# Perceiver block on one core: key weights and chunk 1 moved forward at the start, one accumulator loaded earlier at the end

## The chip, the core and the metric

The kernel runs on 1 core of a Trainium2 chip. The core has TensorE (PE), VectorE (DVE), ScalarE (ACT), GpSimd (POOL) and a sequencer that issues DMAs (SP). They run their own instruction streams and meet through semaphores. Time is device microseconds (us); the kernel before takes 1537.28 us (median of 3 runs, 1536.81 to 1538.84).

## The reference, cut to what matters

Inputs are `x` (8 x 64 tokens of 512) and a context `ctx` (8 x 1601 x 512), all fp32. Three blocks follow each other, each with a residual:

```python
x = x + xattn(layernorm(x), ctx, ctx)   # 16 heads of 32: softmax(Q K^T / sqrt(32)) V, then W_O
x = x + attn(layernorm(x))              # x + differential attention over the heads of a token,
                                        # then layernorm and a 512-2048-512 feed forward with ReLU
x = x + ffn(layernorm(x))               # 32 experts, 6 per token (4 of 8 groups), SwiGLU of 256,
                                        # plus a shared expert of 512
# in xattn:  Q = x_q @ W_Q + b_Q;  K = ctx @ W_K + b_K;  V = ctx @ W_V + b_V
# in ffn:    out = sum over the 6 chosen experts of weight * down(silu(gate(x)) * up(x)) + shared(x)
```

The change lies in the preparation of Q and of the first keys, and in the last sum of `ffn`.

## The kernel before, in words

Matmuls of the cross attention are fp32 products made of three passes: each operand is split into a high part (`*_hi`, rounded to fp32r) and a low part (`*_lo`, the rest), and `mm3` (L65 to L67) adds hi*hi, hi*lo and lo*hi. So every loaded operand needs two instructions before PE can use it: a copy into the high part and a subtraction for the low part.

The context of one batch row is loaded transposed in 4 chunks of 402 columns (`c_raw`, 804 KB each; chunks are numbered 0 to 3). At the start ACT and DVE split chunk 0, and POOL splits chunks 1 to 3 by `split(b, c)` (L294 high, L297 low); POOL waits for `split_done` of chunk 0 first. Key step n (0 to 7) of a half of the heads multiplies chunk n // 2 by 128 columns of W_K: 12 matmuls of 402 columns into PSUM bank n % 3. ACT then adds the bias and rounds (`kT_hi`, L592), DVE makes the low part (`kT_lo`, L733), and that frees the bank: step n waits for the low part of step n - 3.

The queries of all tokens are prepared once. DVE normalises `xn` (statistics L977 to L984, a square root on ACT at L707, L986 to L989), PE transposes it in 16 pieces (L569), ACT and DVE split the transposed `xnT` (L713, L995) and the weights `wq` (L709, L997), and after key step 3 PE makes the projection in 48 matmuls. ACT and DVE split the result (`q_hi` L719, `q_lo` L1012), SP stores it and reads it back in the layout `qbd` (L263, L196). Before `q_hi` the scaled bias `bqs` must be there (L1008), and DVE makes two small selection matrices `sel` (L1000, L1001). The order on each engine is simply the order in which the code is written; nothing is scheduled by a planner. The same holds for the queue of SP, in which the loads are issued one after the other.

Then a loop over 8 batch rows and two halves of the heads does values, scores, softmax and the weighted sum, and in the gaps the key steps of the next half. Two further stages follow: the rest of the second block, and the routing with the experts. In the expert stage PE, DVE, ACT, SP and POOL run a loop of 6 expert blocks of 128 tokens per turn. POOL's scatter (L1691) adds the 128 result rows of a block to one of two accumulators in HBM, `acc0` for even and `acc1` for odd blocks. At the end SP waits for both accumulators (L1665 to L1667), loads four 128-row tiles of each (L1670, 256 KB each), DVE adds the pairs (L1870) and SP stores them (L1673). The tile `part` that receives the loads lies over the expert stage's working tile `e_mix`: `part[:, 0]` over the results `y` of blocks 0 to 3, `part[:, 1]` over the results of blocks 4 and 5 and what follows them.

Of the kernel before, what the change touches and what calls it, by code (L numbers as in the profile page):

```python
# [69 lines left out]
def queries_and_cross_attention(nc, a, keep):  # L70
# [6 lines left out]
    with ExitStack() as ctx:  # L77
# [304 lines left out]
        def _(pe):  # L382
# [181 lines left out]
            pe.wait_ge(ident_loaded, 16)  # L564
            for k in range(KD):
                for t in range(TT):
                    if k == 0:
                        pe.wait_ge(xn_done, t + 1)
                    ins = nc.tensor.transpose(ps[:, 4 + k, P * t:P * t + P], xn[:, t, P * k:P * k + P], ident[:])  # L569
                ins.then_inc(tr_full, 1)  # L570
# [17 lines left out]
        def _(act):  # L588
# [140 lines left out]
        def _(dve):  # L729
# [1418 lines left out]
```

## Time and profile before

| what | value |
|---|---|
| runs of the kernel before | 1537.28 us (1536.81 to 1538.84) |
| profiled execution, its own time | 1538.13 us |
| its span, mean granted clock of PE | 1536.2 us, 0.979 |
| busy: PE, PE weight loads, DVE, ACT, POOL | 95%, 78%, 55%, 36%, 37% |
| c_hi on POOL (L294), 31 of them, mean | 2905 ns |
| kT_lo on DVE (L733), 128 of them, mean | 635 ns |
| kT_hi (L592), q_hi (L719), square root (L707) on ACT at the start | 598, 690, 201 ns |
| bytes: a chunk; x, half of wkv, wq; an accumulator tile | 804 KB; 1024 KB each; 256 KB |
| expert weights w_gu, issue to landing, median of 49; the last | 7.9 us; 7.5 us |
| reload of the queries, 8 DMAs, issue to landing | 2.0, 2.2, 2.4 us (least, median, most) |
| DMA engines busy at 1520-1522, 1522-1524, 1524-1526, 1526-1528 us | 0.97, 0.61, 0.06, 0.96 |

Busy time is the time in which an engine executes. PE's busy time includes pipelined matmuls, whose ends are modelled, so rows of PE are read by their starts. In a timeline, brackets give the idle time before an instruction and what ended it. The mean busy share hides that the two ends of the program look different from the middle.

### The profile page before, as it was taken

How to read it: one execution, taken by the hardware profiler on the slowest of the kernel's cores; microseconds unless marked ns; L12 is line 12 of the kernel's file. 1: busy time of each engine (PE TensorE's matmuls, PEld its weight loads, DVE VectorE, ACT ScalarE, POOL GpSimd, SP SyncE). 2: the span in 40 equal slices, each digit the busy share in tenths (PEclk: the TensorE clock that was granted, in tenths of full speed). 3: DMA queues.
4: the chain of work that ended last, by engine and by line, in shares of the span. 5: the costliest groups of instructions: out<-in, count | busy, mean ns of one | idle time of the engine just before them, and what ended most of it. 6: DMA issues, size and time to landing. Idle time of an engine off the chain costs nothing. (4 is left out here: it accounts for less than half of the span.)

```text
span 1536.2 us, 23747 instructions
## 1 busy us (share of the span) xinstructions
PE 1464.4 (95%) x8826; PEld 1191.7 (78%) x8826; DVE 844.1 (55%) x2161; ACT 549.2 (36%) x1022; POOL 565.4 (37%) x276
## 2 busy tenths in 40 slices
PE   5999999999999999999999999788998989999994
PEld 4999999989999999899989999636665445555552
DVE  6455555544586755488655578739402634444442
ACT  3344345344354354443444533522211012222331
POOL 5006006006366604374811554526400124444442
PEclk9999999999999999999999999989997999999997
DMA  5102003013003013002112200350004659999999
GB/s 197 63 4 90 5 4 121 4 62 94 26 5 97 3 71 118 28 4 65 33 48 92 78 1 1 148 249 1 1 0 158 229 179 333 350 331 341 332 338 301
DMA packets 63976, 176.97 MB, mean 115 GB/s; under 512 B 15110, under 2 KB 32006, under 8 KB 54028
## 3 DMA queue, kind: packets, MB, share of 16 engines
q1 hardware_dynamic: 53708, 151.57, 27.7%
q0 software_dynamic: 10176, 24.12, 6.4%
q8 instruction: 64, 1.05, 0.3%
q14 instruction: 28, 0.23, 0.0%
HBM read 156.00 MB, written 19.66 MB: 114 GB/s over the span
## 5 line engine op out<-in xcount | busy, mean ns | idle before, releaser
L65 PE MATMUL ps_x<-wkv_hi,c_hi 128*128 128x256 f32 (+1 forms) x832 | 241.2, 290 | 0.0
L67 PE MATMUL ps_x<-wkv_hi,c_lo 128*128 128x256 f32 (+1 forms) x832 | 234.2, 282 | 0.0
L66 PE MATMUL ps_x<-wkv_lo,c_hi 128*128 128x256 f32 (+1 forms) x832 | 234.2, 281 | 0.0
L294 POOL TENSOR_TENSOR c_hi<-c_raw,ones 128x1608 fp32r<-128x1608 f32 x31 | 90.1, 2905 | 344.8 <-DMA c_raw<-ctxT 344.8
L769 DVE TENSOR_TENSOR pT<-ps_x,pT 128x512 fp32r<-128x512 f32 (+1 forms) x224 | 145.1, 648 | 123.3 <-ACT pT L617 120.6
L65 PE MATMUL ps_x<-c_hi,wkv_hi 128*128 128x402 f32 x512 | 195.7, 382 | 2.9 <-POOL c_lo L297 2.3
L617 ACT CAST pT<-ps_x 128x512 fp32r<-128x512 f32 (+1 forms) x224 | 124.5, 556 | 167.4 <-PE ps_x L472 164.4
L67 PE MATMUL ps_x<-c_hi,wkv_lo 128*128 128x402 f32 x512 | 177.9, 347 | 0.0
L66 PE MATMUL ps_x<-c_lo,wkv_hi 128*128 128x402 f32 x512 | 177.8, 347 | 0.0
L65 PEld LDWEIGHTS ps_x<-wkv_hi,c_hi 128*128 128x128 f32 (+1 forms) x832 | 153.5, 184 | 17.0 <-issue 17.0
L598 ACT CAST vv<-ps_x 128x512 fp32r<-128x512 f32 (+1 forms) x112 | 62.1, 555 | 278.5 <-PE ps_x L67 278.5
L1937 PE MATMUL ps_e<-e_w_gu,e_xT 128*128 128x512 f32 x344 | 157.1, 600 | 0.0
L67 PEld LDWEIGHTS ps_x<-wkv_hi,c_lo 128*128 128x128 f32 (+1 forms) x832 | 153.6, 185 | 0.0
L66 PEld LDWEIGHTS ps_x<-wkv_lo,c_hi 128*128 128x128 f32 (+1 forms) x832 | 153.2, 184 | 0.0
L313 POOL TENSOR_TENSOR x_tok<-t_q,t_k 128x1024 f32<-128x1024 f32 x48 | 114.2, 2397 | 101.0 <-PE ps_x L524 58.2
L739 DVE TENSOR_TENSOR vv<-ps_x,vv 128x512 fp32r<-128x512 f32 (+1 forms) x112 | 72.9, 651 | 138.9 <-ACT vv L598 138.9
L487 PE MATMUL ps_x<-pT,vv 128*128 128x256 f32 (+1 forms) x832 | 138.0, 287 | 4.8 <-DVE pT L769 4.4
L487 PEld LDWEIGHTS ps_x<-pT,vv 128*128 128x128 f32 (+1 forms) x832 | 125.8, 189 | 10.6 <-DVE pT L769 7.6
L733 DVE SCALAR_TENSOR_TENSOR kT_lo<-ps_x,bk,kT_hi 128x402 fp32r<-128x402 f32 x128 | 81.1, 635 | 95.9 <-ACT kT_hi L592 95.4
L752 DVE TENSOR_SCALAR_CACHE_REDUCE prob<-ps_x 128x402 f32<-128x402 f32 (+1 forms) x256 | 131.2, 569 | 0.0
L472 PE MATMUL ps_x<-ident,prob 128*128 128x128 f32 (+1 forms) x832 | 127.9, 273 | 0.0
L1691 POOL DMA_INDIRECT acc<-e_mix,e_row_out x42 | 66.3, 1579 | 144.7 <-DVE e_row_in L1747 120.7
(314 smaller groups left out, 2685.6 us busy)
## 6 DMA issues: line engine op xcount, KB each, us to landing
e_w_gu<-w_gu SPq DMA_DIRECT2D x49, 1024.0 KB, 7.9
c_raw<-ctxT SPq DMA_DIRECT2D x32, 804.0 KB, 5.0
e_w_dn<-w_dn SPq DMA_DIRECT2D x48, 512.0 KB, 5.6
x_tok<-slabs SPq DMA_DIRECT2D x13, 1024.0 KB, 4.8
spare<-slabs SPq DMA_DIRECT2D x8, 1024.0 KB, 11.1
h_late<-slabs SPq DMA_DIRECT2D x4, 1024.0 KB, 16.6
e_mix<-shared SPq DMA_DIRECT2D x2, 1536.0 KB, 8.5
wkv_raw<-w_qkv SPq DMA_DIRECT2D x2, 1024.0 KB, 12.3
```

Of the source, the lines that this page charges most:

```text
L65: nc.tensor.matmul(out, a_hi, b_hi, start=start, stop=False)
L66: nc.tensor.matmul(out, a_hi, b_lo, start=False, stop=False)
L67: return nc.tensor.matmul(out, a_lo, b_hi, start=False, stop=stop)
L294: nc.gpsimd.tensor_tensor(c_hi[:, :, chunk(c)], c_raw[:, :, chunk(c)], ones[:, 0:1].unsqueeze(2).to_broadcast([P, KD, CW]), ALU.mult).then ...
L313: nc.gpsimd.tensor_tensor(slab[:, 2 * D * (i % 2):2 * D * (i % 2) + 2 * D].rearrange("p (a b d) -> p a b d", a=2, b=2 * H2), q[:, 2 * i:2 ...
L472: ins = nc.tensor.transpose(ps[0:r, 6 + n % 2, c:c + P], prob[:, 2 * g + j, P * st:P * st + r], ident[:])
L487: ins = nc.tensor.matmul(ps[:, 4 + g, 256 * j:256 * j + 256], vv[0:r, st, 2 * g + j].rearrange("p l c -> p (l c)"), pT[0:r, n % 2, st % 2, ...
L617: nc.scalar.copy(pT[0:r, n % 2, 0:w, :, 0].rearrange("p a j c -> p (a j) c"), ps[0:r, 6 + n % 2, 0:256 * w].rearrange("p (a c) -> p a c", ...
L733: nc.vector.scalar_tensor_tensor(kT_lo[:, m, chunk(c)], ps[:, n % KEY_BANKS, 0:CW], bk[:, 2 * h + m:2 * h + m + 1], f32(kT_hi[:, m, chunk( ...
L752: ins = nc.vector.tensor_scalar(prob[:, p, CW * n:CW * n + w], ps[:, 2 * (i % 2) + j, 0:w], 0.0, None, ALU.add, ALU.max, accum_out=pmax[:, ...
L769: nc.vector.tensor_tensor(pT[0:r, n % 2, 0:w, :, 1].rearrange("p a j c -> p (a j) c"), ps[0:r, 6 + n % 2, 0:256 * w].rearrange("p (a c) -> ...
L1937: ins = nc.tensor.matmul(ps[:, GU], xT[:, b, P * g:P * g + P], w_gu[:, b, g], start=(g == 0), stop=(g == KD - 1))
```

## The change: what it does

- SP loads the key half of `wkv_raw` first, then chunk 0 and x; chunk 3 is issued before the value half of `wkv_raw`.
- ACT makes `wkv_hi` first, then the high part of chunk 0, `wq_hi`, the square root and the high part of chunk 1 (which POOL did; POOL leaves it out at (0, 1)). It takes the keys of steps 0 and 1 before `xnT_hi`.
- DVE makes `wkv_lo` first; it takes the keys of steps 0 and 1 right behind the normalised x, then `wq_lo` (which stood behind `xnT_lo`), `xnT_lo`, the keys of steps 2 and 3, and only then `sel`.
- PE does key steps 0 and 1, then the 16 transposes, then key steps 2 and 3.
- At the end SP issues the four loads of `acc0` when `acc0` is complete and `acc1` lacks only its last scatter. The loads of `acc1` follow when the last scatter has landed, each behind the landing of its `acc0` partner.

```diff
@@ sync
+            sp.dma_start(wkv_raw[:, :, 0:D], a["w_qkv"][1]).then_inc(wkv_loaded[0], 16)
             load_chunk(0, 0)
             sp.dma_start(xn[:], a["x"].rearrange("(t p) d -> p t d", p=P)).then_inc(qx_loaded, 16)
-            sp.dma_start(wkv_raw[:, :, 0:D], a["w_qkv"][1]).then_inc(wkv_loaded[0], 16)
...
             load_chunk(0, 2)
+            load_chunk(0, 3)
             sp.dma_start(wkv_raw[:, :, D:], a["w_qkv"][2]).then_inc(wkv_loaded[1], 16)
-            load_chunk(0, 3)
@@ gpsimd, split(b, c)
-                nc.gpsimd.tensor_tensor(c_hi[:, :, chunk(c)], c_raw[:, :, chunk(c)],
-                                        ones[:, 0:1].unsqueeze(2).to_broadcast([P, KD, CW]), ALU.mult).then_inc(split_hi, 1)
+                if (b, c) != (0, 1):
+                    nc.gpsimd.tensor_tensor(c_hi[:, :, chunk(c)], c_raw[:, :, chunk(c)],
+                                            ones[:, 0:1].unsqueeze(2).to_broadcast([P, KD, CW]), ALU.mult).then_inc(split_hi, 1)
@@ tensor (the 16 transposes went behind key step 1)
             for n in range(8):
                 for half in range(2):
                     keys(0, 0, n, half)
+                if n == 1:
+                    pe.wait_ge(ident_loaded, 16)
+                    for k in range(KD):
+                        for t in range(TT):
+                            if k == 0:
+                                pe.wait_ge(xn_done, t + 1)
+                            ins = nc.tensor.transpose(ps[:, 4 + k, P * t:P * t + P], xn[:, t, P * k:P * k + P], ident[:])
+                        ins.then_inc(tr_full, 1)
@@ scalar
+            act.wait_ge(wkv_loaded[0], 16)
+            nc.scalar.copy(wkv_hi[:, :, 0:D], wkv_raw[:, :, 0:D]).then_inc(wkv_hi_done, 1)
             act.wait_ge(c_loaded[0], 16)
             nc.scalar.copy(c_hi[:, :, chunk(0)], c_raw[:, :, chunk(0)]).then_inc(split_hi, 1)
...
+            act.wait_ge(c_loaded[1], 16)
+            nc.scalar.copy(c_hi[:, :, chunk(1)], c_raw[:, :, chunk(1)]).then_inc(split_hi, 1)
             act.wait_ge(bk_loaded, 16)
+            for n in range(2):
+                keys(0, 0, n)
             for m in range(KD):
                 act.wait_ge(tr_full, m + 1)
                 nc.scalar.copy(xnT_hi[:, m], ps[:, 4 + m]).then_inc(xT_hi_done, 1)
-            for n in range(4):
+            for n in range(2, 4):
                 keys(0, 0, n)
@@ sync, the end
-            for i in range(2):
-                wait_turn(sp, added[i], n * (16 * U // 2) + 16)
+            wait_turn(sp, added[0], n * (16 * U // 2) + 16)
+            wait_turn(sp, added[1], n * (16 * U // 2))
+            for t in range(TT):
+                sp.dma_start(part[:, 0, t], a["acc0"][P * t:P * t + P]).then_inc(part_loaded[t], 16)
+            wait_turn(sp, added[1], n * (16 * U // 2) + 16)
             wait_turn(sp, hid_done, n * U + 1)
             for t in range(TT):
-                for i in range(2):
-                    sp.dma_start(part[:, i, t], a[f"acc{i}"][P * t:P * t + P]).then_inc(part_loaded[t], 16)
+                sp.wait_ge(part_loaded[t], 16)
+                sp.dma_start(part[:, 1, t], a["acc1"][P * t:P * t + P]).then_inc(part_loaded[t], 16)
```

ACT at the start of the program, before. `q_std` is the square root, `q_wq_hi` the high part of the query weights, `q_xnT_hi` that of the transposed x.

```order
L703 CAST c_hi<-c_raw 128x4x402 [waits x_c_loaded0]
L705 CAST wkv_hi<-wkv_raw 128x4x512 [waits q_wkv_loaded0]
L707 ACTIVATE q_std<-q_veps 128x4 [waits q_step]
L709 ACTIVATE q_wq_hi<-q_wq_raw 128x2048 [waits q_w_loaded]
L713 CAST q_xnT_hi<-ps_x 128x512 [waits q_tr_full,q_bk_loaded]
L713 CAST q_xnT_hi<-ps_x 128x512 [waits q_tr_full] x3
L592 ACTIVATE kT_hi<-ps_x,bk 128x402 [waits x_k_full] x4
```

The same stretch of ACT, now.

```order
L705 CAST wkv_hi<-wkv_raw 128x4x512 [waits q_wkv_loaded0]
L707 CAST c_hi<-c_raw 128x4x402 [waits x_c_loaded0]
L709 ACTIVATE q_wq_hi<-q_wq_raw 128x2048 [waits q_w_loaded]
L711 ACTIVATE q_std<-q_veps 128x4 [waits q_step]
L713 CAST c_hi<-c_raw 128x4x402 [waits x_c_loaded1]
L594 ACTIVATE kT_hi<-ps_x,bk 128x402 [waits x_k_full,q_bk_loaded]
L594 ACTIVATE kT_hi<-ps_x,bk 128x402 [waits x_k_full]
L719 CAST q_xnT_hi<-ps_x 128x512 [waits q_tr_full] x4
L594 ACTIVATE kT_hi<-ps_x,bk 128x402 [waits x_k_full] x2
```

The weights went ahead of chunk 0, the square root went behind `q_wq_hi`, the copy of chunk 1 came in, and two of the four keys went ahead of `q_xnT_hi`.

DVE behind the statistics of x, before. `q_xn` is the normalised x, `sel` the selection matrices, `bqs` the scaled query bias.

```order
L989 TENSOR_SCALAR q_xn<-q_xn,q_mv,q_rstd 128x512 x3
L992 TENSOR_TENSOR wkv_lo<-wkv_raw,wkv_hi 128x4x512 [waits q_wkv_hi_done]
L995 TENSOR_TENSOR q_xnT_lo<-ps_x,q_xnT_hi 128x512 [waits q_xT_hi_done] x4
L997 SCALAR_TENSOR_TENSOR q_wq_lo<-q_wq_raw,q_wq_hi 128x2048 [waits q_wq_hi_done]
L1000 MEMSET sel 128x64 [waits q_ident_loaded]
L1001 TENSOR_TENSOR sel<-ident 128x64
L1000 MEMSET sel 128x64
L1001 TENSOR_TENSOR sel<-ident 128x64
L733 SCALAR_TENSOR_TENSOR kT_lo<-ps_x,bk,kT_hi 128x402 [waits x_k_hi_done,q_bk_loaded]
L733 SCALAR_TENSOR_TENSOR kT_lo<-ps_x,bk,kT_hi 128x402 [waits x_k_hi_done] x3
L1008 TENSOR_SCALAR bqs<-bq 128x4 [waits q_bq_loaded]
```

The same stretch of DVE, now.

```order
L997 TENSOR_SCALAR q_xn<-q_xn,q_mv,q_rstd 128x512 x3
L739 SCALAR_TENSOR_TENSOR kT_lo<-ps_x,bk,kT_hi 128x402 [waits x_k_hi_done,q_bk_loaded]
L739 SCALAR_TENSOR_TENSOR kT_lo<-ps_x,bk,kT_hi 128x402 [waits x_k_hi_done]
L1005 SCALAR_TENSOR_TENSOR q_wq_lo<-q_wq_raw,q_wq_hi 128x2048 [waits q_wq_hi_done]
L1008 TENSOR_TENSOR q_xnT_lo<-ps_x,q_xnT_hi 128x512 [waits q_xT_hi_done] x4
L739 SCALAR_TENSOR_TENSOR kT_lo<-ps_x,bk,kT_hi 128x402 [waits x_k_hi_done] x2
L1013 MEMSET sel 128x64 [waits q_ident_loaded]
L1014 TENSOR_TENSOR sel<-ident 128x64
L1013 MEMSET sel 128x64
L1014 TENSOR_TENSOR sel<-ident 128x64
L1016 TENSOR_SCALAR bqs<-bq 128x4 [waits q_bq_loaded]
```

`wkv_lo` left this stretch (it stands ahead of the low part of chunk 0 now), the keys went ahead of `sel`, and `q_wq_lo` went ahead of `q_xnT_lo`.

## Rows read from the trace of the kernel before

**Rows 1.** Windows: stretch, its us, busy us of each engine, PEclk, DMA share, GB/s

```profile
100.00:200.00 100.00, 100.00 (x759) 96.56 (x758) 53.23 (x141) 41.84 (x72) 26.08 (x8) 1.00 0.12 37
```

**Rows 2.** Timeline of PE: start, us, engine, line, op, count [idle before, releaser]

```profile
14.78 4.32 PE L569 MATMUL ps_x<-ident,q_xn 128*128 128x128 f32 x16 [14.78 <-DVE q_xn L989]
18.75 0.68 PE L65 MATMUL ps_x<-c_hi,wkv_hi 128*128 128x402 f32 x1
...
19.90 0.54 PE L65 MATMUL ps_x<-c_hi,wkv_hi 128*128 128x402 f32 x1
20.23 0.54 PE L66 MATMUL ps_x<-c_lo,wkv_hi 128*128 128x402 f32 x1
...
26.60 0.45 PE L65 MATMUL ps_x<-c_hi,wkv_hi 128*128 128x402 f32 x1 [2.31 <-POOL c_lo L297]
...
32.73 0.39 PE L65 MATMUL ps_x<-q_xnT_hi,q_wq_hi 128*128 128x512 f32 x1
...
43.61 0.35 PE L65 MATMUL ps_x<-c_hi,wkv_hi 128*128 128x402 f32 x1
...
52.45 0.28 PE L65 MATMUL ps_x<-wkv_hi,c_hi 128*128 128x256 f32 x1
```

**Rows 3.** Timeline of ACT, the start

```profile
5.95 1.53 ACT L703 CAST c_hi<-c_raw 128x1608 fp32r<-128x1608 f32 x1 [3.73 <-DMA c_raw<-ctxT]
11.83 1.90 ACT L705 CAST wkv_hi<-wkv_raw 128x2048 fp32r<-128x2048 f32 x1 [4.35 <-DMA wkv_raw<-w_qkv]
...
14.56 1.91 ACT L709 ACTIVATE q_wq_hi<-q_wq_raw 128x2048 fp32r<-128x2048 f32 x1 [0.72 <-DMA q_wq_raw<-w_qkv]
```

**Rows 4.** Timeline of DVE, the start

```profile
7.51 1.84 DVE L974 TENSOR_TENSOR c_lo<-c_raw,c_hi 128x1608 fp32r<-128x1608 f32 x1 [5.99 <-ACT c_hi L703]
9.26 2.46 DVE L977 BATCH_NORM_STATS2 q_stats<-q_xn 128x6 f32<-128x512 f32 x4
...
14.08 1.92 DVE L989 TENSOR_SCALAR q_xn<-q_xn,q_mv,q_rstd 128x512 f32<-128x512 f32 x4
15.92 2.29 DVE L992 TENSOR_TENSOR wkv_lo<-wkv_raw,wkv_hi 128x2048 fp32r<-128x2048 f32 x1
18.12 2.48 DVE L995 TENSOR_TENSOR q_xnT_lo<-ps_x,q_xnT_hi 128x512 fp32r<-128x512 f32 x4
20.51 2.57 DVE L997 SCALAR_TENSOR_TENSOR q_wq_lo<-q_wq_raw,q_wq_hi 128x2048 fp32r<-128x2048 f32 x1
...
23.08 3.55 DVE L1001 TENSOR_TENSOR sel<-ident 128x64 f32<-128x64 f32 x1
```

**Rows 5.** Timeline of POOL, the start

```profile
17.06 3.87 POOL L294 TENSOR_TENSOR c_hi<-c_raw,ones 128x1608 fp32r<-128x1608 f32 x1 [15.39 <-DMA c_raw<-ctxT]
21.01 5.54 POOL L297 TENSOR_TENSOR c_lo<-c_raw,c_hi 128x1608 fp32r<-128x1608 f32 x1
...
29.45 3.65 POOL L297 TENSOR_TENSOR c_lo<-c_raw,c_hi 128x1608 fp32r<-128x1608 f32 x1
```

**Rows 6.** Windows, one us of key step 2 (PEclk is 0.50)

```profile
28.00:29.00 1.00, 1.00 (x4) 0.99 (x4) 1.00 (x1) 0.00 (x0) 1.00 (x1) 0.50 0.00 0
```

**Rows 7.** Timeline of the DMA queue of SP, the queries' way out and back

```profile
45.31 0.32 SPq L263 DMA_DIRECT2D q_dram<-q_q_hi  x1
...
49.24 5.14 SPq L196 DMA_DIRECT2D qbd<-q_dram  x8
```

**Rows 8.** The end: chain, SP queue, DVE; landings of 39 scatters, then last scatter and loads

```profile
1516.17 8.37 DMA acc<-e_mix,e_row_out
...
1524.76 3.65 SPq L1670 DMA_DIRECT2D e_mix<-acc  x8
...
1533.11 0.69 DVE L1870 TENSOR_TENSOR e_mix<-e_mix 128x512 f32<-128x512 f32 x1 [0.74 <-DMA e_mix<-acc]
...
DMA to landing us min/median/max: 7.3/8.5/9.5
...
DMA to landing us min/median/max: 2.7/4.4/8.4
```

More of the change, by code:

```diff
@@ L562, in unit @@
                 weigh(b, h, 1, NV - 1)
[L564 to L570, printed above, removed]
             for n in range(8):
@@ L701, in _ @@
             nc.scalar.activation(q_std[:], ones[:, 0:TT], ACT.Sqrt)
+            act.wait_ge(wkv_loaded[0], 16)
+            nc.scalar.copy(wkv_hi[:, :, 0:D], wkv_raw[:, :, 0:D]).then_inc(wkv_hi_done, 1)
             act.wait_ge(c_loaded[0], 16)
             nc.scalar.copy(c_hi[:, :, chunk(0)], c_raw[:, :, chunk(0)]).then_inc(split_hi, 1)
-            act.wait_ge(wkv_loaded[0], 16)
-            nc.scalar.copy(wkv_hi[:, :, 0:D], wkv_raw[:, :, 0:D]).then_inc(wkv_hi_done, 1)
+            act.wait_ge(qw_loaded, 16)
+            nc.scalar.mul(wq_hi[:], wq_raw[:], scale).then_inc(wq_hi_done, 1)
             act.wait_ge(q_step, 3)
             nc.scalar.activation(q_std[:], q_veps[:], ACT.Sqrt).then_inc(q_std_done, 1)
-            act.wait_ge(qw_loaded, 16)
-            nc.scalar.mul(wq_hi[:], wq_raw[:], scale).then_inc(wq_hi_done, 1)
+            act.wait_ge(c_loaded[1], 16)
+            nc.scalar.copy(c_hi[:, :, chunk(1)], c_raw[:, :, chunk(1)]).then_inc(split_hi, 1)
             act.wait_ge(bk_loaded, 16)
+            for n in range(2):
+                keys(0, 0, n)
             for m in range(KD):
@@ L972, in _ @@
             nc.vector.memset(f32(zero[:]), 0.0)
+            dve.wait_ge(wkv_hi_done, 1)
+            nc.vector.tensor_tensor(wkv_lo[:, :, 0:D], wkv_raw[:, :, 0:D], f32(wkv_hi[:, :, 0:D]), ALU.subtract).then_inc(wkv_lo_done, 1)
             dve.wait_ge(split_hi, 1)
@@ L990, in _ @@
                                         ALU.mult).then_inc(xn_done, 1)
-            dve.wait_ge(wkv_hi_done, 1)
-            nc.vector.tensor_tensor(wkv_lo[:, :, 0:D], wkv_raw[:, :, 0:D], f32(wkv_hi[:, :, 0:D]), ALU.subtract).then_inc(wkv_lo_done, 1)
+            dve.sem_inc(o_done, 2)
+            dve.sem_inc(pT_lo_done, 14)
+            dve.wait_ge(bk_loaded, 16)
+            for n in range(2):
+                keys(0, 0, n)
+            dve.wait_ge(wq_hi_done, 1)
+            nc.vector.scalar_tensor_tensor(wq_lo[:], wq_raw[:], scale, f32(wq_hi[:]), ALU.mult, ALU.subtract).then_inc(wq_lo_done, 1)
             for m in range(KD):
@@ L995, in _ @@
                 nc.vector.tensor_tensor(xnT_lo[:, m], ps[:, 4 + m], f32(xnT_hi[:, m]), ALU.subtract).then_inc(xT_lo_done, 1)
-            dve.wait_ge(wq_hi_done, 1)
-            nc.vector.scalar_tensor_tensor(wq_lo[:], wq_raw[:], scale, f32(wq_hi[:]), ALU.mult, ALU.subtract).then_inc(wq_lo_done, 1)
+            for n in range(2, 4):
+                keys(0, 0, n)
             dve.wait_ge(ident_loaded, 16)
@@ L1001, in _ @@
                 nc.vector.tensor_tensor(sel[:, j, 64 * j:64 * j + 64], ident[:, 0:64], ident[:, 64:128], ALU.add)
-            dve.sem_inc(o_done, 2)
-            dve.sem_inc(pT_lo_done, 14)
-            dve.wait_ge(bk_loaded, 16)
-            for n in range(4):
-                keys(0, 0, n)
             dve.wait_ge(bq_loaded, 16)
```

## The prediction

> **What bounds the kernel now.** I first read the busy time by stretches of 100 us. A typical row of the attention stage shows PE busy for all of its 100 us, at full clock, with DVE, ACT and POOL at about half or less [rows 1]. So whatever lets PE begin this work earlier should move everything behind it, unless an idle stretch later swallows it. The change touches only the two ends of the program, so I read PE's timeline there. It shows three things [rows 2]: nothing before the query transposes at 14.78 us; an idle 2.31 us (on the chunk-1 low part from POOL) before key step 2 at 26.60; and from the query projection at 32.73 to the first values matmul at 52.45 no gap. Each of the other engines' timelines says what released these points. At the end the reader is to see a chain without PE: the last scatter, eight loads, four adds, four stores [rows 8].
>
> **The start, step by step.** Times are from the span's start.
>
> Loads. Before, the 804 KB chunk 0 landed when ACT began at 5.95; the wkv half, third in the queue, at 11.83; wq at 14.56 [rows 3]; x (1024 KB, second) no later than 9.26, where DVE took it up [rows 4]. So chunk and x together, 1828 KB, landed by 9.26, 1024 KB in 3.3 us. The queue gets the same bytes in another order: wkv lands at about 6.6 (224 KB more than a chunk, 0.7 us), chunk 0 by 9.2, x at 11.8, wq and chunk 1 as before, 14.56 and 17.06 [rows 3, 5].
>
> ACT: wkv_hi 6.6 to 8.5 (1.90), c_hi 9.2 to 10.7 (1.53), wq_hi 14.56 to 16.5 (1.91), the square root to 16.6 (0.2), c_hi of chunk 1 from 17.06 (when it has landed) to 18.6 (1.53, as for chunk 0) [rows 3].
>
> DVE: wkv_lo 8.5 to 10.8 (2.29), c_lo of chunk 0 to 12.7 (1.84), statistics 12.7 to about 15.8 (2.46 and some 0.6 of small instructions), then it waits for the square root, which now stands behind wq_hi; x normalised 16.8 to 18.7 (1.92) [rows 4]. That is later than before (14.08 to 16.0), which is harmless as long as PE has keys 0 and 1 to do.
>
> PE: key steps 0 and 1, 24 matmuls, can start at 12.7. At the slow pace (0.33 us apart, 19.90 to 20.23 [rows 2]: 402 columns at 1.2 GHz) they take 8.0 us; at the fast pace (48 of them from 43.61 to 52.45, 0.184 each [rows 2]) 4.4. Before, PE worked from 14.78 and was slow at 20.23 still. I take half slow, half fast: end at about 19. The bounds are 17.1 and 20.7. The 16 transposes took 3.97 us to the first key matmul before, part of it waiting for x; at most that again: end between 21 and 24.7, likeliest 22.
>
> POOL is what decides. Before: c_hi 3.87, c_lo 5.54, ready at 26.55 [rows 5]. Now c_hi is ACT's and c_lo starts at 18.65; an undisturbed one is 3.65 [rows 5]: ready at 22.3. **Key step 2 starts at 22.4 in place of 26.60, 4.2 earlier.** Its clean length (24 x 0.184 = 4.4) ends at 26.8; before it took 6.1 (26.60 to 32.73), because PE ran at 1.2 GHz for a while after its idle stretch (0.50 of the clock at 28 to 29 [rows 6]). Now the idle stretch is short or none.
>
> The projection also needs wq_lo and four xnT_lo. Here I weigh DVE against POOL. The select instruction of 128x64 elements ran from 23.08 for 3.55 us and ended at 26.63, just after POOL's c_lo (26.55) [rows 4, 5]; and c_lo itself took 5.54, 1.9 more than 3.65, with wq_lo beside it until 23.08. So two-input DVE instructions on SBUF and POOL's exclude each other whole. Then wq_lo, ready at 20.5 (behind keys 0 and 1), waits for POOL until 22.3, takes 2.1 and ends at 24.5; xnT_lo (2.48, from PSUM, 2.48 beside a running POOL before, so not excluded) ends at 27.0. **The projection starts at 27.1 in place of 32.73: 5.6 earlier.** The Trainium skill, page "SBUF — State Buffer", section "SBUF: two separate sides", says that the shared pair is an exclusive lock held for the whole instruction, and that the loser fully blocks; this trace agrees (3.55 us for 64 columns). By a mere sharing of bandwidth the sum would be 26.8, 0.3 better. The page doesn't say who gets the lock at a handover between two queued POOL instructions, which is a rival below.
>
> Query chain. The bqs instruction now stands behind keys 2, 3 and both selects on DVE; the three are SBUF instructions, and POOL runs c_hi, c_lo, c_hi, c_lo from 24.5 on, 2 x (2.9 + 3.65) = 13.1, to 37.6. One slips in at each boundary; bqs may come at 37.6. The four q_hi (0.69) then end at about 40.3, wkv_hi 42.2, wkv_lo 44.4, the low part of key 4 at 45.0. PE does the projection in 10.9 (32.73 to 43.61 [rows 2]), ends at 38.0, and after keys 4, 5 and 6 (2.2 each) wants key 7 at 44.6, whose bank needs that low part: 0.35 lost. Before, DVE had a margin there. The stores and reloads of the queries move from 45.31 to about 41.2, and so the loads from 49.24 to 45.1 [rows 7]; first scores are wanted at about 50.1 (47.2 and 24 matmuls of 256 columns), four loads of 0.64 and the longest landing of the eight, 2.4 (table of the profile), end at 50.1 [rows 7]: just in time. **Start: 5.6 less 0.35, 5.2 us gained** at the first values matmul. Bounds: if all keys and transposes run slow, step 2 starts at 24.7 and keeps its slow stretch: 2 us gained; at best nothing waits: 6.
>
> **The end.** The last scatter is issued at 1516.17 and lands 8.37 later; then eight loads of 256 KB are issued in 3.65, the last add starts at 1533.11 and the kernel ends 3.1 later [rows 8]. The first load lands 2.7 after its issue [rows 8], so seven more take 5.6, 0.80 each. With the change the acc0 loads are issued once the scatter before the last has landed (issued 6.2 earlier, 8.5 to land: about 1518.5), behind the last weight load of 1516.0, which is in at about 1523.7 (7.9 by the page, 7.5 by its own window); 4 x 0.80 later, at 1526.9, they are in. The acc1 loads start at 1524.8, each behind its acc0 partner's landing, so the last is issued at 1527.0 and lands 2.7 later, 1529.7. Against 1533.1 that is 3.4; the four stores come closer together, I take 0.2 off. **End: 3.2 us gained.** DMA engines were busy 0.06 of the time at 1524 to 1526 (table of the profile), so the room is there. What it may cost: the last scatter now shares its last microsecond with loads. With full queues 39 scatters took 7.3 to 9.5, median 8.5, against 8.4 for this one [rows 8]: between 1.1 gained and 1.1 lost, taken as 0.1, inside the rounding. Bounds of the end: 1.5 to 4.4.
>
> By the Trainium skill, "DMA: Bandwidth & Descriptors", section "Queues, rings and completion order", each DMA engine alternates between queues packet by packet; this speaks against the change, since every acc0 packet would delay a scatter packet. The steady scatters above agree that the price is small; if all 1 MB were taken turn by turn with the scatter's tail, it would be one for one at most 256 KB, 0.8 us.
>
> **Sum.** The profiled execution took 1538.13 (span 1536.2 and 1.9 around it), 0.85 above the median of 1537.28. 1538.13 - 5.2 - 3.2 = 1529.7; on the median 1528.9. I say 1529.0. What can be told from no change is 0.2%, 3.1 us, so either half alone is about at that limit.
>
> **Rivals.**
> 1. PE is slow for longer at the start (keys, transposes and again step 2 at 1.2 GHz), or wq_lo loses one handover (2.9 later). For it: the slow pace lasted from 14.78 past 20.23, and after 2.3 idle us it came back [rows 2, 6]. Against: PE now has dense work from 12.7. Start gain about 3: 1531.2. Chance 0.2.
> 2. The end gives nothing: the scatter lands later, or the acc1 loads queue behind acc0 so that the same 2 MB end as late. Against: the idle DMA time. 1537.28 - 5.2 = 1532.1. Chance 0.1.
> 3. The change doesn't do what it says at the start: the chunk-1 copy on ACT stands behind wq_hi and the square root; if x or wq land late (c_hi begins after 19), most of the 4.2 goes. One us of delay costs one. With 3 us of delay, 1532. Chance 0.05.
> 4. The other side. POOL wins every handover: its five instructions run to 22.3 + 13.1 = 35.4 before wq_lo gets in, which ends at 37.5 and xnT_lo at 40.0; the projection starts at 40.1 in place of 32.73, 7.4 lost, 3.2 won at the end: 1541.5. It decides once the projection starts after 35.9 (the end's 3.2). For it: POOL's next instruction is already queued. Against: a waiting select did get in at 26.55 between two POOL instructions. Chance 0.04.
> 5. More than forecast: step 2 and the end at their best ends, 6 and 4.4: 1526.9, and a slow stretch of PE between stages may fall otherwise by a us or two. Chance 0.08.
>
> The forecast has 0.53, its own range is 1527 to 1531. Eight in ten: 1525.5 to 1533.0. Faster by over 0.2% (below 1534.2): the forecast, rivals 1, 2, 3 and 5 less their tails, 0.89. Within 0.2%: 0.06. Slower: 0.05.
>
> **What would show it.** First key matmul at about 12.7 and not after 14; POOL's c_lo from 18.6, 3.7 long; key step 2 at 22.4; wq_lo stretched over POOL's end; first projection matmul at 27.1; bqs ending with a POOL instruction near 37.6; a gap of some 0.4 before key 7; first values matmul at 47.2. From there to the last scatter every row should stand 5.2 earlier; if not, an idle stretch on the way took it. At the end: scatter still 8.4 long, and 8.6 from its landing to the last add become 5.2. Wrong would be a step 2 start after 24.7, a projection start after 29, or a scatter of over 9.5.

## The result: 1527.96 us, and the profile after

| kernel | median us (least to most) | runs |
|---|---|---|
| before | 1537.05 (1536.21 to 1538.84) | 6 |
| changed | 1527.96 (1525.01 to 1529.54) | 6 |

The ratio is 0.9934, 95% interval 0.9923 to 0.9945: 9.1 us faster, where 8.3 had been forecast. The profiled execution took 1529.03 us (span 1527.1, mean granted clock 0.981), 9.10 less than that of before. Four marks divide the span, and a gain can be read off between each two:

| stretch | before | changed | gained |
|---|---|---|---|
| start of the span to the first values matmul | 52.45 | 46.64 | 5.81 |
| from there to SP's first load of `shared` (expert stage) | 1119.23 | 1118.07 | 1.16 |
| from there to the issue of the last scatter | 344.49 | 344.58 | -0.09 |
| from there to the end of the last add | 17.63 | 15.39 | 2.24 |

**The start.** The timeline of PE in the changed kernel (start, us, engine, line, operation, count; in brackets the idle time before it and what ended it) answers to [rows 2]:

```profile
12.32 0.67 PE L65 MATMUL ps_x<-c_hi,wkv_hi 128*128 128x402 f32 x1 [12.32 <-DVE c_lo L982]
...
16.82 0.54 PE L66 MATMUL ps_x<-c_lo,wkv_hi 128*128 128x402 f32 x1
17.15 0.40 PE L67 MATMUL ps_x<-c_hi,wkv_lo 128*128 128x402 f32 x1
17.38 0.34 PE L65 MATMUL ps_x<-c_hi,wkv_hi 128*128 128x402 f32 x1
...
19.05 1.91 PE L574 MATMUL ps_x<-ident,q_xn 128*128 128x128 f32 x16
22.18 0.45 PE L65 MATMUL ps_x<-c_hi,wkv_hi 128*128 128x402 f32 x1 [1.23 <-POOL c_lo L298]
...
26.82 0.47 PE L65 MATMUL ps_x<-q_xnT_hi,q_wq_hi 128*128 128x512 f32 x1
...
37.80 0.35 PE L65 MATMUL ps_x<-c_hi,wkv_hi 128*128 128x402 f32 x1
...
46.64 0.28 PE L65 MATMUL ps_x<-wkv_hi,c_hi 128*128 128x256 f32 x1
```

The keys of steps 0 and 1 start at 12.32 and come 0.335 us apart up to 17.15, then 0.184 to 0.19 apart. Fourteen of the 24 are slow. The transposes take 1.91, half of what they took before. From 22.18 on, nothing is slow and nothing stops up to the values.

ACT, DVE and POOL of the same kernel, which answer to [rows 3], [rows 4] and [rows 5]:

```profile
6.21 1.90 ACT L705 CAST wkv_hi<-wkv_raw 128x2048 fp32r<-128x2048 f32 x1 [3.99 <-DMA wkv_raw<-w_qkv]
8.31 1.53 ACT L707 CAST c_hi<-c_raw 128x1608 fp32r<-128x1608 f32 x1 [0.20 <-DMA c_raw<-ctxT]
...
16.80 1.54 ACT L713 CAST c_hi<-c_raw 128x1608 fp32r<-128x1608 f32 x1 [0.36 <-DMA c_raw<-ctxT]
```

```profile
16.68 1.92 DVE L997 TENSOR_SCALAR q_xn<-q_xn,q_mv,q_rstd 128x512 f32<-128x512 f32 x4
...
20.43 3.85 DVE L1005 SCALAR_TENSOR_TENSOR q_wq_lo<-q_wq_raw,q_wq_hi 128x2048 fp32r<-128x2048 f32 x1
24.20 2.47 DVE L1008 TENSOR_TENSOR q_xnT_lo<-ps_x,q_xnT_hi 128x512 fp32r<-128x512 f32 x4
...
30.85 2.83 DVE L1014 TENSOR_TENSOR sel<-ident 128x64 f32<-128x64 f32 x1
33.60 0.16 DVE L1016 TENSOR_SCALAR bqs<-bq 128x4 f32<-128x4 f32 x1
```

```profile
18.51 3.62 POOL L298 TENSOR_TENSOR c_lo<-c_raw,c_hi 128x1608 fp32r<-128x1608 f32 x1 [16.84 <-ACT c_hi L713]
22.10 4.92 POOL L295 TENSOR_TENSOR c_hi<-c_raw,ones 128x1608 fp32r<-128x1608 f32 x1
27.09 3.67 POOL L298 TENSOR_TENSOR c_lo<-c_raw,c_hi 128x1608 fp32r<-128x1608 f32 x1
30.73 2.87 POOL L295 TENSOR_TENSOR c_hi<-c_raw,ones 128x1608 fp32r<-128x1608 f32 x1
33.68 3.69 POOL L298 TENSOR_TENSOR c_lo<-c_raw,c_hi 128x1608 fp32r<-128x1608 f32 x1
```

Read `q_wq_lo` and POOL together: `q_wq_lo` is ready at 20.43, lies until POOL's `c_lo` ends near 22.1, and then POOL's next instruction (4.92 in place of 2.87) waits until `q_wq_lo` is through at 24.28. The selects and POOL's rows show the same handing over.

**The end.** SP's queue, then the chain of waits and the adds of DVE, which answer to [rows 8]:

```profile
1509.11 0.33 SPq L1640 DMA_DIRECT2D e_w_gu<-w_gu  x1
1512.35 1.80 SPq L1676 DMA_DIRECT2D e_mix<-acc  x4
1518.48 2.20 SPq L1681 DMA_DIRECT2D e_mix<-acc  x4
```

```profile
1503.09 9.20 DMA acc<-e_mix,e_row_out
...
1513.22 6.49 DMA e_mix<-acc
1519.71 0.02 issue
1519.72 3.53 DMA e_mix<-acc
```

```profile
1521.13 1.36 DVE L1881 TENSOR_TENSOR e_mix<-e_mix 128x512 f32<-128x512 f32 x2 [13.71 <-DMA e_mix<-acc]
1523.28 1.40 DVE L1881 TENSOR_TENSOR e_mix<-e_mix 128x512 f32<-128x512 f32 x2 [0.78 <-DMA e_mix<-acc]
```

The scatter before the last lands 9.20 after its issue and releases the `acc0` loads at 1512.35. The last scatter is issued at 1509.29, and the `acc1` loads, which wait for it, start at 1518.48, 9.19 later; before it was 8.59 (1516.17 to 1524.76). The chain then holds no scatter but a load of `acc0` that takes 6.49 and its partner of `acc1` that takes 3.53. So the wait for the partner ended last there, by this profile.

### The profile page after: what moved, and what is told of

The parts are those of the page before. It is cut to its first block and busy times, and to the rows that moved or that the text cites. A ratio compares the mean times of both kernels' runs of the same rounds, so it can differ in the third digit from the quotient of the medians.

```text
span 1527.1 us, 23749 instructions
## 1 busy us (share of the span) xinstructions
PE 1461.4 (96%) x8826; PEld 1189.9 (78%) x8826; DVE 843.1 (55%) x2161; ACT 550.8 (36%) x1023; POOL 561.8 (37%) x275
## 5 line engine op out<-in xcount | busy, mean ns | idle before, releaser
L298 POOL TENSOR_TENSOR c_lo<-c_raw,c_hi 128x1608 fp32r<-128x1608 f32 x31 | 113.5, 3662 | 19.2 <-ACT c_hi L713 16.8
```

What stands on the lines that cost most here:

```text
L298: nc.gpsimd.tensor_tensor(c_lo[:, :, chunk(c)], c_raw[:, :, chunk(c)], f32(c_hi[:, :, chunk(c)]), ALU.subtract).then_inc(split_done, 1)
```

## Experiments

Every kernel here computes the whole reference. The ratio is against before, measured beside it: e1 to e4, e5 to e8, and e9 with e10 were measured together, e11 by itself. Medians of different groups aren't compared, since before took 1536.95 to 1538.19 beside them. The three columns on the right are stretches of one profile each, between the marks of the table above.

| kernel | median us | ratio (95%) | first values | values to `shared` | last scatter to last add |
|---|---|---|---|---|---|
| e1, start alone | 1531.36 | 0.9959 (0.9945 to 0.9973) | 46.34 | 1118.0 | 18.49 |
| e2, end alone | 1534.08 | 0.9985 (0.9975 to 0.9994) | 52.01 | 1117.2 | 15.63 |
| e3, POOL copies | 1537.01 | 1.0001 (0.9992 to 1.0011) | 55.06 | 1118.1 | 15.93 |
| e4, copy alone | 1536.13 | 0.9991 (0.9980 to 1.0001) | 51.52 | 1118.1 | 19.47 |
| e5, no partner wait | 1527.34 | 0.9930 (0.9917 to 0.9942) | 46.43 | 1116.4 | 15.83 |
| e6, no last prefetch | 1526.26 | 0.9921 (0.9908 to 0.9934) | 47.92 | 1120.9 | 12.74 |
| e7, both | 1525.20 | 0.9919 (0.9906 to 0.9932) | 46.58 | 1119.0 | 13.20 |
| e8, changed again | 1527.41 | 0.9932 (0.9917 to 0.9946) | 46.43 | 1118.1 | 15.57 |
| e9, copy and keys | 1531.09 | 0.9967 (0.9954 to 0.9980) | 48.12 | 1116.4 | 18.17 |
| e10, behind the scatter | 1526.43 | 0.9933 (0.9920 to 0.9945) | 46.54 | 1117.4 | 13.19 |
| e11, no prefetch, old end | 1527.05 | 0.9929 (0.9916 to 0.9943) | 46.18 | 1117.7 | 14.48 |

**e1 and e2: the two halves.** e1 is the changed kernel with the old end, e2 the old start with the new end:

```diff
@@ e1, against the changed kernel
-            wait_turn(sp, added[0], n * (16 * U // 2) + 16)
-            wait_turn(sp, added[1], n * (16 * U // 2))
-            for t in range(TT):
-                sp.dma_start(part[:, 0, t], a["acc0"]...)
...
+            for i in range(2):
+                wait_turn(sp, added[i], n * (16 * U // 2) + 16)
@@ e2, against the kernel before: the same lines the other way round
```

> The changed kernel with the end of the kernel before (eight loads behind the last scatter). Theory (the two halves add up, and the part of the gain that fell between them is the PE clock falling differently): key step 2 at 22.2, projection at 26.8, first values matmul at 46.6 as in the changed kernel, last scatter issue to last add 16.9 us as before; time 1537.1 - 5.8 = 1531.3 us, give or take 1.5 for the clock. Rival (the early loads at the end do nothing and the start brings all 9.1): 1528.0. Rival (the extra us between the ends belongs to the start change): first values matmul to last scatter issue is 1462.7 again, against 1463.7 before.

> The kernel before with only the changed end. Theory: the start is that of before (values at 52.5); last scatter issue to last add falls from 16.9 to 14.7 us, of which a later landing of the scatter takes 0.7; time 1537.1 - 2.3 = 1534.8. Rival (the scatter's 9.1 us was chance, the early loads cost it nothing): 14.0, time 1534.1. Rival (the loads cost the scatter more than that in other runs): over 15.5, time 1536 or more.

Measured: 0.9959 and 0.9985. Multiplied they make 0.9944, against 0.9934 and 0.9932 for both halves together: additive within the intervals. By these ratios the start gives about 6.3 us and the end 2.3; by the difference of the medians (1537.07 before, beside them) it is 5.7 and 3.0. The chain of waits of e1, the last lines:

```profile
1508.86 8.56 DMA acc<-e_mix,e_row_out
...
1526.66 0.69 DVE e_mix L1878
```

One profile is a poor measure of the end, because the scatter's length varies. Over the profiles without early loads (before, e1, e4, e9) the last column is 17.63, 18.49, 19.47, 18.17, mean 18.44. With them (changed, e8, e2, e5, e3) it is 15.39, 15.57, 15.63, 15.83, 15.93, mean 15.67. The end is thus worth 2.8 us, and the 2.24 above is low in part because before's own scatter was a short one. From the issue of the last scatter to the first load behind it, the four without early loads take 8.59 to 9.44, mean 8.9, and the five with them 9.19 to 9.79, mean 9.5: the `acc0` loads cost the scatter about 0.6 us, though the two ranges meet.

**e3 and e4: what the copy of chunk 1 on ACT is worth.** e3 gives the copy back to POOL in the changed order; e4 moves only the copy in the old order:

```diff
@@ e3, against the changed kernel
-                if (b, c) != (0, 1):
-                    nc.gpsimd.tensor_tensor(c_hi[...], ...).then_inc(split_hi, 1)
+                nc.gpsimd.tensor_tensor(c_hi[...], ...).then_inc(split_hi, 1)
...
-            act.wait_ge(c_loaded[1], 16)
-            nc.scalar.copy(c_hi[:, :, chunk(1)], c_raw[:, :, chunk(1)]).then_inc(split_hi, 1)
@@ e4, against the kernel before: the same lines the other way round, ACT's copy behind wq_hi
```

> The changed kernel, but the high part of chunk 1 is POOL's again (all orders as changed). Theory (POOL's work for chunk 1 decides key step 2, and POOL and two-input or SBUF-to-SBUF instructions of DVE exclude each other whole): POOL's copy of 2.9 us comes back and wq_lo gets in between copy and subtraction, so c_lo is ready at 26 to 27, key step 2 starts there, the projection at 31 to 32; time about 4.5 above the changed kernel, 1532.5. Rival (the order of PE and DVE brings the gain, the copy on ACT little): key step 2 before 24 and within 1.5 us of the changed kernel's time.

> The kernel before, and only the high part of chunk 1 moves to ACT, behind wq_hi. Theory (exclusion of POOL and DVE): c_lo of chunk 1 is ready at 22.3 and key step 2 starts at 24.2 right behind steps 0 and 1, but DVE's wq_lo ends at 24.4 and the two select instructions, which stand ahead of the keys' low parts, wait for POOL's next two instructions until 27.2 and 30.9; step 3 waits for the low part of step 0 until about 31.6 (30.1 before) and the projection starts at 33.8 to 34.5 (32.7 before): 1 to 2 us slower than before, 1538.5. Rival (POOL alone decides, DVE's order is harmless): projection at 28.7, 4 us faster, 1533.

e3 lost the whole start: first values at 55.06, 2.6 later than before. The profile says why. DVE, then POOL of e3:

```profile
16.50 10.27 DVE L994 TENSOR_SCALAR q_xn<-q_xn,q_mv,q_rstd 128x512 f32<-128x512 f32 x4
26.69 1.17 DVE L736 SCALAR_TENSOR_TENSOR kT_lo<-ps_x,bk,kT_hi 128x402 fp32r<-128x402 f32 x2
27.78 4.61 DVE L1002 SCALAR_TENSOR_TENSOR q_wq_lo<-q_wq_raw,q_wq_hi 128x2048 fp32r<-128x2048 f32 x1
```

```profile
16.74 3.03 POOL L294 TENSOR_TENSOR c_hi<-c_raw,ones 128x1608 fp32r<-128x1608 f32 x1 [15.07 <-DMA c_raw<-ctxT]
19.85 3.64 POOL L297 TENSOR_TENSOR c_lo<-c_raw,c_hi 128x1608 fp32r<-128x1608 f32 x1
23.45 3.04 POOL L294 TENSOR_TENSOR c_hi<-c_raw,ones 128x1608 fp32r<-128x1608 f32 x1
26.57 3.68 POOL L297 TENSOR_TENSOR c_lo<-c_raw,c_hi 128x1608 fp32r<-128x1608 f32 x1
```

Four instructions of 0.48 each took 10.27 us: one before POOL began, and each of the other three waited out one of POOL's instructions. PE stood for 3.39 and 2.53 us between the transposes, and key step 2 came at 29.52. I had expected the normalisation, which has one tensor input, to be untouched; it is excluded too. The profile of before had already shown this in `bqs`, also an instruction with one input: its 16 bytes per partition, 0.16 us in the changed kernel, took 1.84 beside POOL's copy (33.05 to 35.92):

```profile
34.12 1.84 DVE L1008 TENSOR_SCALAR bqs<-bq 128x4 f32<-128x4 f32 x1
```

The prediction let `bqs` be excluded, but did not ask the same of the normalisation. By the Trainium skill, "SBUF — State Buffer", section "SBUF: two separate sides", a DVE operation in a two-port mode takes the lock as well as one with two SBUF inputs; e3 fits that, though no trace here names the mode of an instruction. So in the changed order the copy on ACT is worth 8.4 to 8.6 us at the first values (55.06 against 46.64 and 46.43), not 4.5.

I had expected e4 to be 1 to 2 us slower than before. It was 0.9 us earlier at the first values (51.52 against 52.45), and its time can't be told from before's. Step 2 came at 23.23 without idle time, 3.4 earlier, but most of that was lost again. PE at step 3, then DVE, of e4:

```profile
27.91 0.45 PE L65 MATMUL ps_x<-c_hi,wkv_hi 128*128 128x402 f32 x1 [2.34 <-DVE kT_lo L736]
```

```profile
21.28 3.08 DVE L1000 SCALAR_TENSOR_TENSOR q_wq_lo<-q_wq_raw,q_wq_hi 128x2048 fp32r<-128x2048 f32 x1
...
24.36 2.81 DVE L1004 TENSOR_TENSOR sel<-ident 128x64 f32<-128x64 f32 x1
...
27.16 0.16 DVE L1004 TENSOR_TENSOR sel<-ident 128x64 f32<-128x64 f32 x1
27.24 1.71 DVE L736 SCALAR_TENSOR_TENSOR kT_lo<-ps_x,bk,kT_hi 128x402 fp32r<-128x402 f32 x3
```

The keys' low parts stand behind the selects, which wait for POOL, so PE waits 2.34 for a bank. This is the mechanism that I had named for e4, but it was too small to make e4 slower than before, because the second select took 0.16: it got in between POOL's copy (to 27.09) and the subtraction behind it (27.16). A second cost came behind the wait: from 29.11 to 32.38 the matmuls of PE are at the slow pace (PEclk is 0.50 at 30 to 32 us). Nine of them took 3.27 us, where nine at the fast pace take 1.8, so 1.5 us of the loss is the clock's.

**e9: the copy, and the keys' low parts ahead of the selects, in the old order of loads and of PE.**

```diff
@@ e4's edit, and in DVE's program
-            dve.wait_ge(ident_loaded, 16)
-            for j in range(2):
-                nc.vector.memset(sel...); nc.vector.tensor_tensor(sel...)
...
             for n in range(4):
                 keys(0, 0, n)
+            dve.wait_ge(ident_loaded, 16)
+            for j in range(2):
+                nc.vector.memset(sel...); nc.vector.tensor_tensor(sel...)
```

> The kernel before with two things of the change: the high part of chunk 1 on ACT, and DVE takes the four keys' low parts ahead of the select instructions (loads, PE's order, weights and the end as before). Theory (these two carry the start's gain; the earlier weights and the keys ahead of the transposes mainly fill time that PE has anyway): step 2 at 23.2 right behind steps 0 and 1, step 3 without a wait at 25.4, projection at 27.7, first values matmul at 47.5: 5.0 of the 5.8 us; time 1532.3. Rival (loading and splitting the weights first is what counts): projection not before 30, time within 2 us of the kernel before.

Measured: 1531.09 for 1532.3 forecast, and first values at 48.12, 4.3 earlier than before (e1 was 6.1 earlier). In e9 steps 2 and 3 begin at 24.02 and 26.20 and neither waits for anything; PE is simply busy with keys 0 and 1 until 24.0, since it began them at 18.72. So two small edits bring 4.3 of 6.1. The rest must come from the other edits of the start (the key weights first, keys ahead of the transposes, the other orders on ACT and DVE); none of them was tried by itself, and the ratios of e9 and e1 (0.9967, 0.9959) overlap.

**e5 to e8: the partner wait and the useless weight loads.** e5 takes away the wait of each `acc1` load for its partner (both increments then meet in one semaphore, which DVE awaits at 32). In e6 SP's last turn doesn't load expert weights for a turn that never comes. e7 has both; e8 is the changed kernel, once more.

```diff
@@ e5
-                sp.wait_ge(part_loaded[t], 16)
@@ e6 (PE's waits at the end are lowered to match)
-            with sp.Fori(0, n) as i:
+            with sp.Fori(0, n - 1) as i:
```

> The changed kernel without SP's wait for the acc0 tile before each acc1 load (the add still waits for both). In the changed kernel the last two acc0 tiles landed at 1519.7 and 1520.3, after the scatter (1518.4), and held the last two acc1 loads back. Theory (the queue of loads is the limit, the wait costs what it delays the last load): last acc1 load issued 0.4 to 0.6 us earlier, last scatter issue to end of the last add 15.0 in place of 15.4 to 15.9; time 0.5 below the changed kernel, within noise. Rival (the DMA engines are full until then anyway): no difference.

> The changed kernel, but SP's loop of expert weight loads runs one turn less: it no longer loads, in the last turn, 12 weight tiles for blocks that don't exist. Theory (the last scatter takes 8.4 to 9.8 us and the early acc0 loads 6 to 6.6 us because they stand in full DMA queues): with empty queues the scatter lands in 4 to 6 us, acc0 is in before that, and only 2.6 + 3 x 0.8 us of acc1 loads follow: last scatter issue to end of the last add about 11 in place of 15.4 to 15.9, time 4.5 below the changed kernel, 1523.5. Rival (the scatter's time is its own, a read and a write behind each other): it still takes over 8 us, and only the two late acc0 tiles are won: 14.5, time 1527. Rival (weight traffic also slows PE's loop): first shared load to last scatter falls below 344.4.

> The two edits of the run before and this one together: no useless weight loads in the last turn and no wait for the acc0 tile. Theory: with empty queues acc0 is in long before, so the wait costs nothing there: the same as without the useless loads alone, 11 us from the last scatter issue to the last add's end, 1523.5. Rival (the wait instructions themselves cost issue time): 0.2 less.

> The changed kernel again on the chip of these runs, as their yardstick. Theory: 1528 give or take 1.5; first values matmul at 46.6, last scatter issue to end of the last add 15.4 to 15.9; from the first values matmul to the first shared-expert load 1117 to 1119 as the clock falls. Rival (the middle stretch is fixed by the start's order): 1118.1 again within 0.1.

e5 is 0.9930 beside e8's 0.9932, with 15.83 and 15.57 at the end: the partner wait costs nothing that can be measured. In e5 the last pair of adds starts 14.5 us behind the scatter's issue (1507.22 to 1521.70), in the changed kernel 14.0. The chain of the changed kernel named that wait because it came last, which doesn't make it the bound; only taking it away shows that.

e6 and e7 show that the weight loads do cost time at the end. The last scatter in the chain of e6:

```profile
1509.48 6.00 DMA acc<-e_mix,e_row_out
```

That is 6.0 (6.5 in e7) in place of about 9, and scatter to last add is 12.74 and 13.20 in place of 15.6: 2.4 to 2.9 us. The whole time doesn't show it clearly. In the medians e7 is 2.2 and e6 1.2 below e8 (1525.20 and 1526.26 against 1527.41), but the intervals overlap, and e10, which leaves out the same loads, has the ratio of e8 (0.9933). The 4.5 that I expected of e6 is missed: the end came to 12.74 (13.20 in e7), where I had 11 for both. The profile of e6 also lost time at its start; its windows at step 2 (PEclk is the column behind the busy times):

```profile
22.00:24.00 2.00, 1.84 (x6) 1.81 (x7) 2.00 (x1) 0.00 (x0) 2.00 (x2) 0.65 0.52 175
24.00:26.00 2.00, 2.00 (x7) 1.98 (x7) 2.00 (x5) 0.00 (x0) 2.00 (x1) 0.50 0.00 0
```

PE had been idle for 1.85 us before step 2 and the clock fell to 0.50. In the changed kernel's profile it was idle 1.23 and the clock stayed. The length of the idle stretch alone doesn't decide: the clock also stayed up after 1.53 idle us in e10 and after 3.45 in e2. The slow matmuls cost e6 1.3 to 1.5 us at the first values (47.92 against 46.64 and 46.43). The early part is the same program as the changed kernel's, and e6 is the only one of eight profiles with this start in which it happened.

The four stretches of e6 add up only with one that the table leaves out. From `shared` to the last scatter e6 took 340.69 us and e4 342.92, all others 344.39 to 344.58. That isn't the missing weight loads, as a rival in my expectation of e6 would have it, since e7, e10 and e11 leave them out too and took 344.46, 344.39 and 344.50. In e6 all of the difference lies ahead of the first scatter, where the clock fell otherwise: from 10 to 20 us behind `shared` PEclk is 0.66 in e6 and 0.51 in e8.

**e10 and e11: what the early loads are worth without the weight loads.** e10 is e7 with the `acc0` loads put behind the issue of the last scatter. e11 is e6 with the old end.

```diff
@@ e10, against e7
+            wait_turn(sp, sent, n * U)
             for t in range(TT):
                 sp.dma_start(part[:, 0, t], a["acc0"]...)
...
                                              in_=y[:, r % U], ...).then_inc(added[r % 2], 16)
+                pool.sem_inc(sent, 1)
```

> The changed kernel without the useless weight loads and without the wait for the acc0 tile, and now SP issues the acc0 loads only when POOL has issued the last scatter. Without weight loads a scatter took 4.9 us, but the last one 6.0 and 6.5 with the acc0 loads issued just ahead of it. Theory (packets of the loads stand in the scatter's way only when they are in front): scatter back to about 5, acc0 in by the time it lands or 0.5 later, last scatter issue to end of the last add 12.0 in place of 12.7 to 13.2; time 1 us below the same kernel without this edit, 1524.5. Rival (any load in flight costs the scatter the same): scatter 6 to 6.5 and acc0 later, 13.5 or more.

> The changed start, no useless weight loads in the last turn, and the end of the kernel before (eight loads behind the last scatter). It gives the last scatter alone. Theory (without weight loads a scatter takes 4.9 us, and what the last one took beyond that, 6.0 to 7.0, was the price of the acc0 loads in flight): scatter 4.9, last scatter issue to end of the last add 4.9 + 0.2 + 8.6 + 0.7 = 14.4, so that the early acc0 loads are worth 1.2 to 1.7 us here, against 1.9 to 2.9 beside weight loads. Rival (the last scatter is slow for another reason): 6 or more again, 15.5 or more.

SP's queue and the scatter of e10, then the chain of e11:

```profile
1508.24 0.81 SPq L1677 DMA_DIRECT2D e_mix<-acc  x2
```

```profile
1508.36 7.02 DMA acc<-e_mix,e_row_out
```

```profile
1508.42 4.87 DMA acc<-e_mix,e_row_out
...
1522.21 0.69 DVE e_mix L1878
```

e10 failed as an experiment on order: SP was released 0.12 us before the recorded start of the scatter, so the loads still went first. Its 13.19 is e7's 13.20, and its time of 1526.43 misses the 1524.5 that I expected. Whether loads that really follow the scatter would leave it alone stays open.

e11 gives the last scatter by itself: 4.87 us. The scatter before the last, beside which SP issues no loads in e6 and e7, agrees: there the `acc0` loads that wait for it are issued 4.97 and 5.16 behind it. In one window inside the scatter e11 moved 20 GB/s, and the changed kernel 322 in the same window:

```profile
1509.00:1511.00 2.00, 0.00 (x0) 0.00 (x0) 0.00 (x0) 0.00 (x0) 1.00 (x1) 1.00 0.37 20
```

```profile
1509.00:1511.00 2.00, 0.00 (x0) 0.00 (x0) 0.00 (x0) 0.00 (x0) 1.58 (x1) 1.00 1.07 322
```

So a scatter takes 4.9 alone, 6.0 to 7.0 with the 1 MB of `acc0` in flight, and 8.4 to 9.6 among weight loads. The early loads cost it 1.1 to 2.1 us where it would be alone and 0.6 where it is slow anyway. By the last column they are worth 14.48 less 12.74 to 13.20, 1.3 to 1.7 us, in the first case (one profile against three) and 2.8 in the second: the gain of this edit is larger beside the useless loads, since these delay the scatter, and `acc0` is loaded during that delay. The whole times can't tell e11 (0.9929) from e6, e7 and e10 (0.9919 to 0.9933).

## Why the prediction was right, point by point

- **Loads.** The key half of wkv landed at 6.21 (forecast 6.6) and chunk 0 at 8.31 (9.2), so the first keys came at 12.32 for 12.7.
- **Keys 0 and 1, transposes.** Half slow, half fast was taken; 14 of 24 were slow. End 19.05 for 19. The transposes took 1.91 and not 3.97: all 16 had their input and a fast PE. It changed nothing, because PE then waited 1.23 for POOL.
- **Key step 2.** POOL's `c_lo` ran from 18.51 for 3.62, and step 2 started at 22.18 for 22.4. The slow stretch behind it was absent, as forecast; e6 shows that it can come back.
- **wq_lo and the projection.** `wq_lo` waited for POOL and ended at 24.28 (24.5), `xnT_lo` at 26.67 (27.0), and the projection began at 26.82 (27.1). Rival 4, by which POOL wins every handover, is refuted for the changed order: POOL lost to `wq_lo` at 22.1 and to the selects after it. e3 shows its relative, DVE losing all it could.
- **The gap before key 7 did not come**, 0.35 forecast. This step of the working failed: I let `bqs` lose a handover of its own and come at 37.6. It came at 33.60, right behind the second select. Between POOL's copy and its subtraction lies a wait on a semaphore and about 0.08 us, and there not one but several queued short instructions of DVE get in (33.60 in the changed kernel, 27.16 in e4).
- **Queries.** The reloads were issued at 43.45, 1.7 before my 45.1, since the rest came earlier, and first scores had what they needed.
- **Start in all**: 5.81 for 5.2 in this profile: the projection came 0.3 earlier than forecast, and the 0.35 before key 7 wasn't lost. The other profiles with this start have 5.9 to 6.3, but e6 4.5. The old start varies too: e2's first values came at 52.01, since PE was not slow after its wait of 3.45 us there, as it was in the kernel before (PEclk 0.50 at 28 us).
- **The middle** was taken as unchanged. Up to 974 us SP's loads all stand 5.7 to 5.9 earlier, against 5.2 forecast. Behind that the lead went down to 4.3 at 1002 us and up to 7.0 at `shared`, so that a further 1.1 was won in sum, but by chance. A window in each of the two profiles, before and then changed, with PEclk 0.83 and 1.00:

```profile
1070.00:1080.00 10.00, 7.64 (x39) 6.15 (x40) 4.76 (x9) 4.62 (x13) 5.06 (x5) 0.83 0.00 0
```

```profile
1064.00:1074.00 10.00, 7.18 (x44) 5.51 (x45) 4.75 (x9) 4.63 (x13) 4.60 (x5) 1.00 0.00 0
```

The clock fell at other moments. The column "values to `shared`" is 1119.2 (before), 1117.2 (e2), 1118.1 (e4) and 1116.4 (e9) with the old start, and 1116.4 to 1120.9 with the new one. From the first values to the last scatter e1 took 1462.5, as a rival in my expectation of it had it if the extra us belonged to the new start, against 1463.7 before. But e2, e4 and e9 with the old start have 1461.6, 1461.1 and 1461.0. So that is no effect of the change, and it was in rival 5 as a possibility of a us or two.
- **The end**: 2.24 in the profile, 2.8 over five profiles against four, for 3.2. Two terms were off. The scatter's price was taken as 0.1 and measured as 0.6. And from the first `acc1` load to the last add the profile has 5.5 us (1518.48 to 1523.98), where the working had 4.9 (1524.8 to 1529.7). One `acc0` load of the chain took 6.49 us, with the last weight load (issued at 1509.11) and the scatter in flight beside it; I had 0.80 per tile in turn.
- **The rule of the queues.** I bounded the price of the loads at 0.8 by letting them run turn by turn with the scatter's tail. In this change the measured 0.6 is within that bound. Where the scatter has only them beside it, the price is 1.1 to 2.1 (e6, e7, e10 against e11). By the Trainium skill, "DMA: Bandwidth & Descriptors", section "Queues, rings and completion order", each DMA engine alternates between the queues that have work, packet by packet; these runs agree with it in sign, but my bound under it doesn't hold there. For this change what counted is that I took 0.1 and not something near the bound: half a us.
- **Sum.** The start and the middle gave more than forecast and the end less: 5.2 + 3.2 = 8.4 forecast, 5.8 + 1.1 + 2.2 = 9.1 in the profile. The 1.1 of the middle is luck, and it made up for the 1.0 that was missing at the end of this profile. So the time came near the forecast partly by chance; the mechanisms of the start and of the end are those forecast.
- **Rivals 1, 2 and 3** did not happen: no lasting slow stretch (except in e6), an end that gives 2.3 by e2's ratio, and ACT's copy begun at 16.80.

## What to carry to other kernels

Where a gap of PE is closed, follow every instruction of the waiting engines past the next boundary of the engine that excludes them: here the copy alone gave 0.09% (interval 0 to 0.2%), and the copy with the keys' low parts ahead of two tiny selects gave 0.33% (0.2 to 0.46%). Give the copy that stands on a shared resource to an engine that does not use it, before touching the order of the loads. At the end of a kernel, look for loads that no one will use: here the stretch from the last scatter to the last add was 2.4 to 2.9 us shorter without them, in three profiles, while the loads that were moved under the scatter cost it 0.6. The whole times were too noisy to confirm the 2.4 to 2.9.

## What the runs showed of the hardware that I had not expected

- A DVE instruction with a single fp32 tensor input, in place in SBUF (0.48 us for 128 x 512), is shut out by POOL's two-input instructions: three of four lost a whole POOL instruction each, 10.27 us in place of 1.92 (e3). Before's row of `bqs` (1.84 us for 128 x 4) had shown it for a small one.
- Between POOL's copy and the subtraction that waits for it on a semaphore the rows show about 0.08 us, and in it get a waiting DVE instruction and short ones of 0.11 to 0.16 us behind it (33.60 in the changed kernel, 27.16 in e4). Of instructions of 0.48 us only one got in (e3). That the semaphore wait makes this room is read from the rows and was not tested.
- A scatter of 128 rows that adds into HBM takes 4.87 us on quiet queues (e11) and up to 9.6 on full ones (e2), for the same bytes.
- A semaphore that POOL raises behind its scatter instruction is seen by SP before that scatter's recorded start (1508.24 against 1508.36), so the loads didn't get behind the scatter.
- PE's matmuls ran 0.335 us apart from 12.32 to 17.15 while the granted clock of 13 to 17 us is recorded as 1.00. At the first microseconds of the program the pace of the rows has to be read, and not the clock's column:

```profile
13.00:17.00 4.00, 4.00 (x13) 3.96 (x13) 2.60 (x10) 2.21 (x3) 0.00 (x0) 1.00 1.04 355
```

- The clock's falls come at other moments in each execution. The same stretch of about 1118 us took 1116.4 to 1120.9. From the first values to the last scatter, where such falls partly make up for each other, the profiles have 1460.8 to 1463.7. Runs of the changed kernel are spread over 4.5 us (1525.01 to 1529.54).
